# Four reorderings in the attention and expert phase of a decoder layer: where the last batch's norm, the last normalised tile, the ReLUs and the first scores stand

## What is computed

```
q, k, v = project(x1), project(ctx), project(ctx)
x2  = layernorm(x1 + softmax(q k / 4) v Wo + bo)            # xt
w   = softmax of the two best of x2 @ gate_W                # wgt, 4 per token
for e in 4 experts:
    h = relu(layernorm(x2 @ W1[e] + b1[e]) * g1[e] + be1[e])
    y = layernorm(h @ W2[e] + b2[e]) * g2[e] + be2[e]
    acc += w[e] * y
out = layernorm(2 * x2 + acc)                               # the "final" norm
```

## Time and profile before

| what | us |
|---|---|
| median of 3 runs | 1657.34 (1655.27 to 1657.67) |
| the profiled execution, whole | 1650.65 |
| its span (first to last instruction) | 1648.7 |
| busy in the span: VectorE, TensorE, ScalarE, GpSimd | 1408.0, 1316.0, 1123.0, 1024.4 |
| from the first score matmul of turn 1 to that of turn 2 | 1140.93 to 1308.06 |

### The profile page before, as it was taken

One profiled execution on the slowest core, in us unless ns is written; L12 is line 12 of the kernel. 1 busy time (PEld: TensorE's weight loads), 2 busy tenths in 40 slices (PEclk: granted clock), 3 DMA queues, 4 the chain that ended last, 5 costly groups with the idle time before them and its releaser, 6 DMA issues. The chain is left out here.

```text
span 1648.7 us, 22427 instructions
## 1 busy us (share of the span) xinstructions
PE 1316.0 (80%) x7436; PEld 920.8 (56%) x7436; DVE 1408.0 (85%) x2530; ACT 1123.0 (68%) x2548; POOL 1024.4 (62%) x711
## 2 busy tenths in 40 slices
PE   6788788777887787788777879889988998897870
PEld 4566566656666666666555644456445644462460
DVE  5899999999999999999997856597869786978678
ACT  5877888888789878988886523348534853475570
POOL 2799899999999999999988511003700370027025
PEclk9988999999999998999997979999999999999995
DMA  6101210221022102211210023000010000000000
GB/s 206 68 1 68 81 63 20 81 81 62 21 82 81 53 30 81 81 34 48 75 70 31 20 105 118 1 1 1 26 56 1 0 26 26 1 1 1 26 1 25
DMA packets 44581, 76.40 MB, mean 46 GB/s; under 512 B 3825, under 2 KB 38226, under 8 KB 40242
## 3 DMA queue, kind: packets, MB, share of 16 engines
q1 hardware_dynamic: 44466, 74.98, 13.1%
HBM read 66.06 MB, written 8.91 MB: 45 GB/s over the span
## 5 line engine op out<-in xcount | busy, mean ns | idle before, releaser
L974 POOL TENSOR_TENSOR state_c<-state,c_area 128x1024 f32<-128x1024 f32 x256 | 600.7, 2362 | 28.7 <-DVE state L1051 23.6
L1051 DVE TENSOR_TENSOR_SCAN state<-decay,ps 128x512 f32<-128x512 f32 x416 | 503.6, 1213 | 15.6 <-ACT decay L729 14.2
L729 ACT ACTIVATE decay<-step_area,negA 128x255 f32<-128x255 f32 x832 | 351.6, 497 | 0.5 <-DVE step_area L1129 0.5
L1662 POOL TENSOR_TENSOR big<-big,g_sb 128x1024 f32<-128x1024 f32 x29 | 79.4, 2739 | 404.4 <-ACT big L1551 402.7
L1019 DVE TENSOR_TENSOR ps<-step_area,ps 128x512 f32<-128x512 f32 x416 | 283.6, 682 | 16.9 <-PE ps L410 14.6
L426 PE MATMUL ps<-ident_sb,state_c 128*128 128x128 f32 x2048 | 288.7, 290 | 0.7 <-POOL state_c L974 0.7
L426 PEld LDWEIGHTS ps<-ident_sb,state_c 128*128 128x128 f32 x2048 | 257.0, 151 | 25.7 <-issue 12.9
L943 POOL TENSOR_TENSOR ub<-step_area,b_bc 128x1024 f32<-128x1024 f32 x48 | 113.5, 2364 | 27.9 <-DVE step_area L1132 27.9
L1510 PE MATMUL ps<-w_sb,hT 128*128 128x256 f32 x512 | 120.3, 389 | 2.5 <-ACT hT L1620 1.9
L1051 DVE TENSOR_TENSOR_SCAN state<-ps,ub 128x512 f32<-128x512 f32 x96 | 116.1, 1209 | 6.6 <-ACT ps L742 6.1
L1475 PE MATMUL ps<-w_sb,weights 128*128 128x512 f32 x256 | 121.0, 608 | 0.0
(11 more groups left out here) (214 smaller groups left out, 2476.5 us busy)
## 6 DMA issues: line engine op xcount, KB each, us to landing
c_area<-bc_scratch SPq DMA_DIRECT2D x32, 1024.0 KB, 7.9
b_bc<-bc_scratch SPq DMA_DIRECT2D x16, 384.0 KB, 4.6
weights<-in_xT SPq DMA_DIRECT2D x16, 256.0 KB, 3.2
res<-in_x SPq DMA_DIRECT2D x16, 256.0 KB, 2.8
x_scratch<-res SPq DMA_DIRECT2D x16, 256.0 KB, 2.1
weights<-x_scratch SPq DMA_DIRECT2D x4, 1024.0 KB, 9.0
xa<-x_scratch SPq DMA_DIRECT2D x4, 1024.0 KB, 5.7
out_x<-acc SPq DMA_DIRECT2D x4, 1024.0 KB, 4.8
```

The source lines that it names most:

```text
L729: nc.scalar.activation(decay_tile(i, n)[:, j, 1:], dt_sb[:, i[1] % 2, j, 1:], ACT.Exp, scale=negA[:, j * NS + n:j * NS + n + 1]).then_inc( ...
L974: nc.gpsimd.tensor_tensor(state_c[:, n % RING, :, :], state[:, n % RING, :, :], c_bc[:, q, n, :].unsqueeze(1).to_broadcast([P, CT, TC]), A ...
L1051: nc.vector.tensor_tensor_scan(state[:, n % RING, pair, :].rearrange("p j n -> p (j n)"), a, b, 0.0, ALU.mult, ALU.add).then_inc(s_scan, 1)
```

## The change

Five edits, all in `attn_ffn_block`:

- The finished batch's norm (`final_stats`, aggregate, guess, newton, `final`) leaves stage 2. It gets tiles of its own (`fstats` and so on, 8 columns) and stands behind the four early rounds: statistics and variance ahead of `gate_scores`, newton and `final` behind it, the ScalarE part behind `preset(0)` and `preset(1)`.
- `weigh_tile` of the first half-tile no longer stands ahead of `exps(0)`; the pieces move back by one step, and four instead of three are left behind the loop.
- In stage 3 `normalise(0, 3)` stands at t = 7 ahead of `measure` of tile 6 and of the last `round_neg`.
- In stage 4 `guess(b, 2)` stands behind the first eight ReLUs, and of the second half's eight ReLUs four stand ahead of the copy of tile 3 and four between it and `preset(13)`.
- `scores(0)` of turns 1 to 3 begins with heads 0 and 1 (banks 0 and 1) and the remainder once tile 6 has been copied out; heads 2 and 3 wait for tile 7. In turn 0 the order inside is the same, without those waits.

```diff
@@ TensorE, scores
                     if u == 0:
                         pe.wait_ge(s_qm, b * NL + NL)
                         if tail:
+                            pe.wait_ge(s_l2c, b * TT - 1)
+                        pair(0).then_inc(s_s2, 1)
+                        rest()
+                        if tail:
                             pe.wait_ge(s_l2c, b * TT)
+                        pair(1).then_inc(s_s2, 2)
                     else:
                         pe.wait_ge(s_exp, b * 3 * U + 3 * (u - 1) + 2)
...
+                        pair(0)
+                        pair(1).then_inc(s_s2, 2)
+                        rest().then_inc(s_s2, 1)
@@ ScalarE
-                if tail:
-                    weigh_tile(b - 1, *left.pop(0))
                 for u in range(U):
...
                 preset(0)
                 preset(1)
+                if tail:
+                    final_guess(b - 1)
...
-                guess(b, 2)
+                def evict(t):
...
                 for n in range(NT):
                     for c in range(E * KT):
...
+                        if n and c == E * KT // 2 - 1:
+                            evict(TG * n - 1)
+                    if n:
+                        preset(TT + TG * n + 1)
+                    else:
+                        guess(b, 2)
                     for i in range(TG):
                         t = n * TG + i
+                        if i == TG - 1 and n + 1 < NT:
+                            continue
+                        evict(t)
@@ VectorE
                 for t in range(TT):
...
-                    if tail:
-                        final_stats(b - 1, t, TT + t)
-                aggregate(b, 0, cols)
-                newton(b, 0, cols)
+                aggregate(b, 0, TT)
+                newton(b, 0, TT)
...
-                if tail:
-                    final(b - 1, TT)
                 work = rounds() if more else []
                 for r in range(EARLY if more else 0):
                     one_round(b + 1, work.pop(0), base=0)
+                if tail:
+                    for t in range(TT):
+                        final_stats(b - 1, t)
+                    final_aggregate(b - 1)
                 gate_scores(b)
+                if tail:
+                    final_newton(b - 1)
+                    final(b - 1)
...
                     advance(2 * t)
+                    if t == TT - 1:
+                        normalise(0, TG - 1)
...
-                    if t >= TG:
+                    if TG <= t < TT - 1:
                         normalise(0, t - TG)
```

More of the change, by code:

```diff
@@ L1190, in attn_ffn_block @@
         newt = sb("newt2", [P, TG * E])
+        fstats = sb("fstats", [P, TT, 6])
+        fmean = sb("fmean", [P, TT])
+        fvar = sb("fvar", [P, TT])
+        flnv = sb("flnv", [P, TT])
+        frstd = sb("frstd", [P, TT])
+        fnewt = sb("fnewt", [P, TT])
         raw_sc = sb("raw_sc", [P, TT, BLK])
@@ L1243, in attn_ffn_block @@
         s_sum = sem("a_sum")
+        s_fst = sem("a_fst")
+        s_fmv = sem("a_fmv")
+        s_fnw = sem("a_fnw")
+        s_fln = sem("a_fln")
         s_fin = sem("a_fin")
@@ L1250, in attn_ffn_block @@
         STB = TG * E
[L1251 removed]
+        NWB, LNB, NMB, MVB = 5 * NORMS, 2 * NORMS, 6 * NORMS, TT + STB * (NORMS - 1)
         KVB, GDB, ACB = 2 + 2 * HG, 12, TT * (E + 1)
@@ L1394, in scores, with pair, rest @@
                     tokens = slice(half * HALF, (half + 1) * HALF)
+                    def pair(i):
+                        for j in range(2 * i, 2 * i + 2):
+                            rows = slice(BLK * j, BLK * (j + 1))
+                            last = nc.tensor.matmul(ps[:, j, :], kT[rows, g, 0:SM], qT[rows, g, tokens], start=True, stop=True)
+                        return last
+                    def rest():
+                        return nc.tensor.matmul(ps[:, 4 + 3 * (u % 2), :], kTr[:, g, :], qT[:, g, tokens], start=True, stop=True)
                     if u == 0:
@@ L1397, in scores @@
                         if tail:
+                            pe.wait_ge(s_l2c, b * TT - 1)
+                        pair(0).then_inc(s_s2, 1)
+                        rest()
+                        if tail:
                             pe.wait_ge(s_l2c, b * TT)
+                        pair(1).then_inc(s_s2, 2)
                     else:
                         pe.wait_ge(s_exp, b * 3 * U + 3 * (u - 1) + 2)
-                    for j in range(HG):
-                        rows = slice(BLK * j, BLK * (j + 1))
-                        last = nc.tensor.matmul(ps[:, j, :], kT[rows, g, 0:SM], qT[rows, g, tokens], start=True, stop=True)
-                    last.then_inc(s_s2, 2)
-                    nc.tensor.matmul(ps[:, 4 + 3 * (u % 2), :], kTr[:, g, :], qT[:, g, tokens],
-                                     start=True, stop=True).then_inc(s_s2, 1)
+                        pair(0)
+                        pair(1).then_inc(s_s2, 2)
+                        rest().then_inc(s_s2, 1)
                 def values(u):
@@ L1534, in query, with final_guess, guess @@
                                      scale=HD ** -0.5, bias=bqk_sb[:, g:g + 1]).then_inc(s_qc, 1)
-            def guess(b, n, count=2 * TT):
-                cols = count if n in (0, NORMS) else STB
+            def final_guess(b):
+                act.wait_ge(s_fnw, 5 * b + 1)
+                nc.scalar.activation(flnv[:, :], fvar[:, :], ACT.Ln).then_inc(s_fln, 1)
+                act.wait_ge(s_fln, 2 * b + 1)
+                nc.scalar.activation(frstd[:, :], flnv[:, :], ACT.Exp, scale=-0.5).then_inc(s_fln, 1)
+            def guess(b, n):
+                cols = STB if n else TT
                 act.wait_ge(s_nw, b * NWB + (5 * n + 1))
@@ L1592, in turn @@
                     copy_transposed(b + 1, x1T, 4, s_xt, s_xtc)
-                    guess(b, 0, cols0)
+                    guess(b, 0)
                     for u in range(U):
@@ L1612, in turn @@
                         guess(b, 1)
-                guess(b, 2)
+                def evict(t):
+                    act.wait_ge(s_l2, b * TT + t + 1)
+                    nc.scalar.activation(big[:, t // TG, t % TG, :].rearrange("p (a n) -> p a n", a=2),
+                                         ps[:, 2 * (t % 2):2 * (t % 2) + 2, :], ACT.Copy).then_inc(s_l2c, 1)
                 for n in range(NT):
@@ L1637, in turn @@
                         weigh_tile(b, NT - 1, i, range(E))
-                    guess(b, 5, TT)
+                    final_guess(b)
             nc.scalar.preload_act_table_set("natural_log_exp_and_others")
@@ L1770, in normalise, with final_stats, final @@
                 last.then_inc(s_n1, 1)
[L1772 removed]
+            def final_stats(b, t):
                 dve.wait_ge(s_sum, b * TT * E + E * (t + 1))
[L1774 to L1776 removed]
+                nc.vector.bn_stats(fstats[:, t, :], acc[:, t, :]).then_inc(s_fst, 1)
+            def final(b):
                 for t in range(TT):
[L1778 to L1779 removed]
+                    nc.vector.tensor_scalar(acc[:, t, :], acc[:, t, :], fmean[:, t:t + 1], frstd[:, t:t + 1],
+                                            ALU.subtract, ALU.mult).then_inc(s_fin, 1)
             def gate_scores(b):
@@ L1952, in last_tail @@
                 for t in range(pooled, TT):
-                    nc.vector.bn_stats(stats[:, t, :], acc[:, t, :]).then_inc(s_st, 1)
+                    nc.vector.bn_stats(fstats[:, t, :], acc[:, t, :]).then_inc(s_fst, 1)
                 for t in range(pooled):
-                    final_stats(b, t, t)
-                aggregate(b, NORMS, TT)
-                newton(b, NORMS, TT)
-                final(b, 0)
+                    final_stats(b, t)
+                final_aggregate(b)
+                final_newton(b)
+                final(b)
             dve.sem_inc(s_out, 16)
-            dve.sem_inc(s_st, TT)
             turns(dve, turn)
```

40 lines of the change are left out of this document (28 added, 12 removed).

## The result

| kernel | median, us | ratio to before |
|---|---|---|
| before (same chip) | 1657.51 (1655.27 to 1659.65) | |
| changed | 1642.26 (1640.92 to 1647.0, 4 runs) | 0.9914 [0.9894, 0.9935] |
| changed, second group | 1642.15 (1639.86 to 1645.4, 5 runs), before 1651.77 | 0.9941 [0.9928, 0.9955] |

A forecast was written before the change was run, and what follows sets the result against it. No engine is full; the bound is a chain changing hands between engines, at places where TensorE waits. Terms 8.6 + 2.7 + 5.2 + 1.2 - 1.1 = 16.6 off the median 1657.34 give 1640.7 us; range 1633 to 1650.

The forecast's parts named there:

- ReLUs first, turns 0 to 2: Stage 4, first half: earlier transposes and ReLUs gain 2.0 where the clock falls, 4.6 where it stays; 8.6 us in all.
- Turn 3: Stage 4, first half of turn 3: first ReLU comes at 1560.7 instead of 1563.36, a gain of 2.7 us.
- Copy behind four ReLUs: Stage 4, second half: ReLUs start ahead of the copy, net gain 1.3 us in each of four turns, 5.2.
- Scores by half: Start of attention, turns 1 to 3: first exponential 1.3 us earlier, 0.4 of it remaining per turn; 1.2 us.
- Turn 0: Start of attention in turn 0, scores(0) in halves: nothing counted, 0 us.
- Norm: Additions to rounds: moving the finished batch's norm gains 0.2 in turns 1 and 2, loses 1.5 in turn 3; -1.1 us.
- number 4: Ahead of x2: GpSimd later than thought, two more tiles left; 27 us lost against 17.7 gained, 1667; chance 0.05.
- Number 2: Head starts handed on less well: second-half ReLUs give nothing, clock falls three times; gain 8, 1649; chance 0.21.
- Number 1: VectorE and GpSimd hardly meet, or clock never falls: both gain 32 us, 1625; either 22 to 27; chance 0.17.
- Number 3: Stage 4, second half: late normalise becomes TensorE's wait and eats 3.9 in 4 turns; gain about 1, 1656; chance 0.05.

The follow-up runs named there:

- e8: The changed kernel, unedited, run and profiled again in the second group: 1642.15 us, ratio 0.9941.
- e1: Changed kernel with the four heads of scores(0) issued together again, behind the last copy, in every turn: 1639.0 us, ratio 0.9899.
- e4: Changed kernel with the half-tile of weigh_tile back ahead of exps(0), nothing else: 1633.99 us, ratio 0.986.
- e6: e5, but in turns 1 to 3 heads 0 and 1 first, then heads 2 and 3, remainder last: 1622.62 us, ratio 0.9825.
- e9: e5 with the last round_neg directly behind normalise at t = 7, ahead of the measure of tile 6: 1623.45 us, ratio 0.983.
- e10: e6 with e9's edit, the last round_neg ahead of the measure of tile 6: 1622.77 us, ratio 0.9807.
- e5: Changed kernel with the weigh_tile half-tile back ahead of exps(0) and scores(0) whole in every turn: 1624.19 us, ratio 0.9841.
- e7: Kernel before with only the copy of tile 3 behind four second-half ReLUs and preset(13) behind eight: 1648.37 us, ratio 0.995.
- e2: Kernel before with only guess(b, 2) behind the first eight ReLUs and tile 3 normalised ahead of the last round_neg: 1644.87 us, ratio 0.9936.
- e11: Changed kernel with GpSimd's product and additions for tiles 4 to 7 cut to 2 columns, output part left out: 1626.63 us, single run.
- e3: Kernel before with the move of the finished batch's norm alone, weigh_tile's half-tile still ahead of exps(0): 1644.64 us, ratio 0.9939.

## Why the prediction was right

The median came out 1.6 us above the forecast, and the gain in the same group is 15.3. But the second group and the profile pair give 9.6 and 10.3 (8.2 with the untouched part) against 16.6, and the second profile of the changed kernel (e8) 14.8 against the same profile of the kernel before. So the steps are taken one by one, measured in the profile pair, with e8's value where the clock made it another.

- **ReLUs first, turns 0 to 2: 8.6 forecast, 11.39 measured** (3.49, 4.71, 3.19). The clock fell in two turns and stayed in one, as chosen. 4.6 was 4.71; at the lower clock 2.0 was too small, it was 3.2 and 3.5. The forecast took over the price of a fall from the earlier trace rows, 2.07 and 0.5 more, but in the changed kernel a fall costs 1.1 to 1.2 (56.95 and 56.89 against 55.78), since the clock is back sooner: granted 0.79 over the 8 us from the transposes, where the kernel before has 0.72 over the 12 us around turn 1's. In other profiles it stayed up in one, two or all three turns: the choice was right for this pair and no rule.
- **Turn 3: 2.7 forecast, 1.89 measured.** e1, e4, e6, e8, e9 and e10 have 36.10 or 36.11, which is 2.74. The missing 0.8 is the clock in the first expert matrix of that turn: it was low at its start after the change and in e5 (36.92), and up in e8, which is the changed kernel again.
- **Copy behind four ReLUs: 5.2 forecast, 6.15 measured**, 1.54 in every turn. e7 has 1.54 by itself. That it also goes with a clock that stays up in the second half, which e2 lost there (21.61), was not foreseen.
- **Scores by half: 1.2 forecast for turns 1 to 3, nothing measured.** The stretch lost 0.63 a turn, from packed(6), which was booked under the norm with 1.2; e1 shows the split itself at 0.1. The forecast let the exponential start right behind the copy, but TensorE needs as long for two heads as for four, and has the remainder behind.
- **Turn 0: 0 forecast, -5.05 measured.** This is the step that failed outright: "Turn 0: nothing counted". I read the order inside scores(0) as free because no wait was added. The split makes three slots where there were two, at half clock 2.08 each, and a pause of 1.12. The clock then rises late: 13.1 to 13.4 us behind the first score matmul in the four profiles with the split in turn 0 (after, e4, e8, e11), 3.2 to 6.5 in the nine without it. That stretch is 42.5 to 42.6 in the former and 36.4 to 37.7 in the latter. No row of the kernel before that stands ahead of the prediction shows this place, and that was the omission: I looked at turn 1's scores only.
- **Norm: -1.1 forecast, measured -4.13.** It has two parts: packed(6), -3.6 forecast and -1.89 measured, and from the addition to gate_scores +2.5 forecast and -2.24 measured (-0.47, -0.38, -1.39). The path was right: addition to x2 forecast 11.45, measured 11.50; statistics inside the gate wait, 0.5 forecast to spare, 0.49 measured; `final` 1.4 to spare, 1.45. Even the first maximum came where it was forecast, 22.45 behind the first addition by the prediction's frame and 22.41 measured. What was missed is the clock behind it. TensorE reaches the first round 2.2 us earlier than before, so it now waits 2.17 for keys that come no earlier, the clock falls to 0.59, and rounds that took 13.13 take 15.03 and 14.35. Where it stayed up (turn 2 of e8) they take 13.40, and the turn gains 1.16, near the 1.4 forecast. In turn 3 the gate's matmul ran at half clock (1.93 for 1.07), and in e8 it did not: 20.54 and 19.68 against 19.15. By e8's profile the part from the addition to gate_scores is +0.2 and the whole term -1.7. e3 and e4 give the cause its name: with the piece ahead of exps(0), the same move of the norm gains 3.2 in turns 1 and 2 instead of losing 0.4, and 1.5 in turn 3 instead of losing 1.4. GpSimd's work left was sized well: 4.6 forecast at the end of the additions and 4.9 measured, a hold of 3.0 on VectorE forecast and 3.0 measured.

Stage 4 gave 19.4 where 16.5 were forecast (21.4 by e8), everything else -9.1 instead of +0.1 (-6.6 by e8). So the total came near the forecast by errors of opposite sign: stage 4 gave more, and turn 0 took a loss that no term had. The direction, the place of the gain and the range were right; the agreement of the median to 1.6 us is partly the spread of the kernel before, whose profiled run lay 6.7 under its first median and 1.1 under that of the second group.

The Trainium skill ("SBUF — State Buffer", "Who interferes with whom") was cited for VectorE and GpSimd excluding one another. This case's traces agree: 2.29 against 0.42 for one `packed`, and 11.50 against 8.46 for the chain once GpSimd's instructions are two columns wide. The same section of the Trainium skill also says that an instruction with at most one SBUF input doesn't contend outside certain modes; the additions with one operand in PSUM take 0.38 with GpSimd at work, which agrees.

Of the rivals, number 4 (GpSimd late, 27 us lost) had the right mechanism, but only 4.1 of its 27 us lie in it, 1.7 by e8. Number 2 had a gain of 3.3 to 12, where the profile pair and the second group lie, but for another reason: it had the second half's ReLUs give nothing, and they gave 6.15. Number 1, a chain without GpSimd and a clock that never falls, did not come about in the changed kernel; e10, where the clock stays up and the chain is within 1 us of turn 0's, gains 32.9 in the medians, and the rival had said 32; as e10 has three edits that the rival didn't, the match of the numbers is luck. Number 3 fell: `newton(b, 2)` never held up the second half.

Open: what decides whether the clock falls at a given pause (at 2.8 us it stayed in turn 1 and fell in turns 0 and 2 of one execution; and the prediction's anchor, that it is kept at 2.30, failed in turn 3 of e7), and why the state-space part varies by 6 us between profiles, which is as much as the two groups differ.

## What to carry to other kernels

When a piece of work is moved to give another engine a head start, look first at who shares a port or a queue with the engine that gets it later: here one `weigh_tile` placed a step back cost 8.3 us in the medians and 6.5 to 11 in the traces, while the whole change gained 9.6 to 15.3. Price a split of a matmul group by what the halves take in the trace, not by half the whole. And treat a wait of TensorE as a risk of more than its length: behind waits of 1.56 and 2.17 us in this kernel the granted clock was 0.50 and 0.59 in some turns, and stayed at 1.00 behind the same waits in others. So profile a kernel twice before a few us are put down to an edit: the changed kernel's two profiles differ by 4.5 us from the first score matmul to the end.

## What the runs showed of the hardware

- Four matmuls of 32 rows take TensorE as long as eight: 1.13 against 1.14 at 2.4 GHz, 2.08 against 2.09 at 1.2 GHz.
- The granted clock behind a pause is not decided by the pause alone. Ahead of the transposes of stage 4 it fell at 3.76 us in nine of nine turns, at 2.82 in 14 of 24, at 2.38 in none of six, and in turn 3 at 2.30 in one of three. At the wait for the keys, 2.13 to 2.17, it fell in four of six. At 1.56 between the two long runs it fell in turns 0 to 2 of e2 and in none of the eight turns of the kernel before and e3.
- What a fall costs differs too: 2.0 us for the stretch from the transposes to the long run in the kernel before (10.88 in turn 1, 8.88 in turn 3, which kept it), 1.1 in the changed one (8.22 and 7.10).
- A chain of small dependent VectorE instructions beside GpSimd is not held until GpSimd is done: single ones take 1.67 or 0.7 and those between them 0.16, and the eleven ahead of x2 took 3.0 us more in all (first addition to x2 11.50 against 8.46).
